# Routing the first group of the last mixture-of-experts phase inside the attention cycles ahead of it

## The reference

```
x = x + tanh(g_xattn[3]) * attention3(layernorm(x), ctx)      # phase 6
x = x + tanh(g_ffn[3])   * moe3(layernorm(x))                 # phase 7, the last

# moe3: 32 experts of 64 hidden units, in 8 groups of 4
scores = sigmoid(h @ gate_w.T);  sc = scores + gate_bias
group_scores = sum of the top 2 of each group; keep the best 4 groups
masked = sc where kept, else 0;  tki = top 8 of masked
tkw = scores[tki] / (sum + 1e-20) * 2.5
out = sum over experts of tkw * ((silu(h w_gate) * (h w_up)) w_down) + shared expert
```

## Time and profile before

| | |
|---|---|
| three timed runs | 866.33, 873.83, 873.89 us; median 873.83 |
| the profiled execution | 869.13 us, its span 867.3 us, so 1.8 us lie around the span |
| TensorE busy | 824.7 us (95%) |
| VectorE, GpSimd, ScalarE busy | 515.7, 471.2, 407.0 us |
| mean granted TensorE clock | 0.985 of full speed |

### The profile page before, as it was taken

One profiled execution on the slowest core, in us unless ns is written; L12 is line 12 of the kernel. 1 busy time (PEld: TensorE's weight loads), 2 busy tenths in 40 slices (PEclk: granted clock), 3 DMA queues, 4 the chain that ended last, 5 costly groups with the idle time before them and its releaser, 6 DMA issues.

```text
span 867.3 us, 13578 instructions
## 1 busy us (share of the span) xinstructions
PE 824.7 (95%) x4427; PEld 560.2 (65%) x4427; DVE 515.7 (59%) x1444; ACT 407.0 (47%) x730; POOL 471.2 (54%) x449
## 2 busy tenths in 40 slices
PE   5999999998899999999998999999999988999997
PEld 5866676665566666665765666656566665666664
DVE  6866645584865646335555868686755466556431
ACT  2343353634436242325666676756556633424231
POOL 5585757465573747476444343354545248475553
PEclk9999999999999999999999999999999899999999
DMA  8303111214313142441323131322223024424251
GB/s 317 104 15 99 63 36 32 85 43 154 119 44 119 62 129 67 136 124 35 89 83 107 46 89 42 95 50 50 55 49 93 1 67 134 147 66 148 75 154 50
DMA packets 44727, 75.29 MB, mean 87 GB/s; under 512 B 8977, under 2 KB 9361, under 8 KB 44529
## 3 DMA queue, kind: packets, MB, share of 16 engines
q1 hardware_dynamic: 44512, 74.42, 28.4%
q10 hardware_dynamic: 144, 0.01, 0.0%
HBM read 56.11 MB, written 1.51 MB: 66 GB/s over the span
## 4 chain that ended last, share of the span: by engine, by line
PE 56%; DVE 9%; ACT 3%; issue 2%; POOL 0%; ACTq 0%; DVEq 0%; POOLq 0%
PE Y L930 13%; PE B L857 6%; PE B L855 6%; PE B L856 6%; PE B L1498 5%; PE B L1517 3%; PE B L1479 3%; PE B L1485 2%; PE Y L1370 2%; PE B L1478 2%; DVE mxh L1768 1%; PE T L1303 1%; DVE xhat L1752 1%; DVE bcs L1943 1%; ACT shared L1379 1%
## 5 line engine op out<-in xcount | busy, mean ns | idle before, releaser
L1172 POOL TENSOR_TENSOR shared<-shared,bcs 128x512 f32<-128x512 f32 x192 | 247.4, 1293 | 195.8 <-DVE shared L1209 177.0
L1209 DVE TENSOR_TENSOR shared<-shared,B 128x512 f32<-128x512 f32 x204 | 139.5, 686 | 206.4 <-PE B L857 160.4
L1058 ACT ACTIVATE shared<-B 128x512 f32<-128x512 f32 x204 | 121.7, 598 | 280.0 <-PE B L857 279.5
L930 PE MATMUL Y<-shared,down_lo 128*128 128x512 f32 x408 | 209.1, 598 | 0.0
L1712 POOL TENSOR_TENSOR shared_r<-shared_r,const 128x512 fp32r<-128x512 f32 (+1 forms) x128 | 116.4, 940 | 80.3 <-PE B L1479 61.8
L1768 DVE TENSOR_REDUCE mxh<-B 128x4 fp32r<-128x512 f32 (+1 forms) x128 | 78.9, 618 | 82.2 <-PE B L1479 81.5
L1648 ACT COPY shared<-B 128x512 f32<-128x512 f32 (+1 forms) x128 | 64.7, 505 | 61.6 <-PE B L1498 61.5
L1638 ACT ACTIVATE shared<-B 128x512 f32<-128x512 f32 (+1 forms) x128 | 69.6, 544 | 48.9 <-PE B L1485 47.6
L930 PEld LDWEIGHTS Y<-shared,down_lo 128*128 128x128 f32 x408 | 72.5, 190 | 21.1 <-issue 9.5
L855 PE MATMUL B<-shared_r,gate_hi 128*128 128x512 f32 x102 | 80.9, 794 | 0.0
L855 PE MATMUL B<-x_lo_r,gate_hi 128*128 128x512 f32 x102 | 77.6, 761 | 0.4 <-ACT shared L1058 0.4
(11 more groups left out here) (306 smaller groups left out, 1469.8 us busy)
## 6 DMA issues: line engine op xcount, KB each, us to landing
bcs<-wrow SPq DMA_DIRECT2D x96, 256.0 KB, 3.8
shared_r<-shared_r SPq DMA_DIRECT2D x256, 64.0 KB, 2.0
bcs<-wrow SPq DMA_DIRECT2D x128, 128.0 KB, 2.9
gate_lo<-in_moe SPq DMA_DIRECT2D x9, 256.0 KB, 5.3
up_lo<-in_moe SPq DMA_DIRECT2D x9, 256.0 KB, 5.5
down_lo<-in_moe SPq DMA_DIRECT2D x9, 256.0 KB, 4.3
small<-in_small SPq DMA_DIRECT2D x1, 1372.5 KB, 11.7
X<-in_x SPq DMA_DIRECT2D x4, 256.0 KB, 5.2
```

The lines of the kernel that those rows point to most:

```text
L930: nc.tensor.matmul(Y[:], w_raw[2][:, at:at + P], hid[(n0 + c) % HIDDEN], start=(i == 0), stop=(i == m["NC"] - 1))\
L1058: nc.scalar.activation(sg[(n0 + n) % ACTIVE], B[n % GATES][:], ACT.Silu).then_inc(sem("sg_ready"), 1)
L1172: gp.tensor_tensor(hid[(n0 + n) % HIDDEN], hid[(n0 + n) % HIDDEN], bcs[(PLACE.k0[p] + r // m["PER"]) % BROADCAST], ALU.mult)\
L1209: nc.vector.tensor_tensor(hid[(n0 + n) % HIDDEN], sg[(n0 + n) % ACTIVE], up[:], ALU.mult)\
```

## The change

Group 0 of phase 7 is taken through everything up to its router row before the second stream begins. In cycle 6 DVE takes its statistics at t = 10 and applies them at t = 14, POOL's power for it is moved behind the key spreading of the next cycle's first quarter. In cycle 7 a new table `FINAL` puts `rows` at t = 1 and `result` at t = 15, and `ROUTE` puts the low part at t = 2, the logits at 3, an exponential on ACT at 4, the seven pieces of the routing on DVE at 5 to 11, the turn at 12 and the row's copy at 13. The sigmoid of this one group becomes exp(-x) on ACT, and an addition of 1 and a reciprocal on DVE. Group 1's statistics come at t = 14 of cycle 7 in place of chunk 4. In the stream, `xt` of group 1 moves from chunk 7 to chunk 1 and its logits from chunk 9 to 6; the leftovers of phase 6 shift from chunks 1, 2, 3 to 3, 4, 5. Context lines are cut:

```
@@ -640,6 +640,11 @@
             dve.wait_ge(sem("logits_read"), PLACE.no[p] + g + 1)
+            if (p, g) == (7, 0):
+                st.add(v.tensor_scalar(t["sig"][:], t["sig"][:], 1.0, None, ALU.add))
+                st.settle()
+                st.add(v.reciprocal(t["sig"][:], t["sig"][:]))
+                st.settle()
             st.add(v.tensor_tensor(t["s"][:].rearrange("p (j n) e -> p j (n e)", j=GB), t["sig"][:],
@@ -701,7 +706,7 @@
                     if (p, g) == (7, 0):
-                        table.update(xt=7, logits=9)
+                        table.update(xt=1, logits=6)
                     if (p, g) == (1, 0):
@@ -991,23 +996,24 @@
                         back_pe(pe, 6, QUADS * NG - 1)
-                    elif (p, n) == (7, 1):
-                        pe.wait_ge(sem("logits_read"), PLACE.no[7] + 1)
+                    elif (p, n) == (7, 3):
+                        pe.wait_ge(sem("x_lo_ready"), PLACE.no[7] + 2)
                         upsample_pe(pe, NG - 1)
-                    elif (p, n) == (7, 2):
+                    elif (p, n) == (7, 4):
                         pe.wait_ge(sem("up_ready"), NG)
                         heads_turned_pe(pe, 6, NG - 1)
-                    elif (p, n) == (7, 3):
+                    elif (p, n) == (7, 5):
                         output_pe(pe, 6, NG - 1)
-                    elif (p, n) == (7, 5):
-                        turn(7, 0)
                 G = run.hook("xt", n)
...
                     p, g = run.groups[G]
-                    pe.wait_ge(sem("w_row_ready"), PLACE.no[p] + g + 1)
+                    if (p, g) == (7, 0):
+                        pe.wait_ge(sem("x_updated"), s - 1)
+                    else:
+                        pe.wait_ge(sem("w_row_ready"), PLACE.no[p] + g + 1)
                     normed(s + 1)
@@ -1022,6 +1028,8 @@
                     pe.wait_ge(sem("x_lo_ready"), PLACE.no[p] + g + 1)
+                    if (p, g) == (7, 1):
+                        pe.wait_ge(sem("heads_oT_ready"), CYCLES)
                     logits(p, g)
@@ -1058,12 +1066,10 @@
                     turned_act(act, 1)
-                elif (p, n) == (7, 2):
+                elif (p, n) == (7, 4):
                     heads_turned_act(act, 6, NG - 1)
-                elif (p, n) == (7, 4):
+                elif (p, n) == (7, 6):
                     result_act(act, 6, run.step(0) - 1)
-                elif (p, n) == (7, 6):
-                    turned_act(act, 7)
                 H = run.hook("xt", n - 1)
@@ -1193,8 +1199,7 @@
             else:
-                pieces = route_dve(dve, st, 7)
-                next(pieces)
+                pieces = iter(())
             setup = setup_dve(dve, st)
@@ -1210,12 +1215,8 @@
                     divided_dve(dve, st, 6, QUADS * NG - 1)
-                elif (p, n) == (7, 1):
+                elif (p, n) == (7, 3):
                     upsample_dve(dve, NG - 1)
-                elif (p, n) == (7, 4):
-                    norm_stats(st, 1)
-                if (p, g) == (7, 0):
-                    next(pieces, None)
                 for kq, what in (("q", "query"), ("k", "key")):
@@ -1453,8 +1454,11 @@
 
+        FINAL = dict(rows=1, key=8, query=11, result=15, value=4)
+        ROUTE = dict(low=2, logits=3, exp=4, first=5, turn=12, row=13)
+
         def steps_of(c):
-            return LATER if c else FIRST
+            return FIRST if c == 0 else LATER if c + 1 < CYCLES else FINAL
 
@@ -1524,7 +1528,7 @@
                 else:
-                    pe.wait_ge(sem("heads_oT_ready"), c)
+                    pe.wait_ge(sem("x_updated"), S4 + c - 1)
                 pe.wait_ge(sem("xhat_ready"), S4 + c + 2)
@@ -1535,7 +1539,7 @@
                 else:
-                    pe.wait_ge(sem("xhat_t_ready"), S4 + c + 2)
+                    pe.wait_ge(sem("w_row_ready"), PLACE.no[7] + 1)
                 for j in range(GB):
@@ -1556,7 +1560,7 @@
                         else:
-                            pe.wait_ge(sem("x_updated"), S4 + c - 1)
+                            pe.wait_ge(sem("logits_read"), PLACE.no[7] + 1)
                         upsample_pe(pe, c - 1 - NG)
@@ -1592,9 +1596,11 @@
                         values_pe(pe, *group(c + 1))
-                    if t == 15 and c + 1 == CYCLES:
-                        pe.wait_ge(sem("x_updated"), S4 + c)
+                    if t == ROUTE["logits"] and c + 1 == CYCLES:
                         route_pe(pe, 7)
+                    if t == ROUTE["turn"] and c + 1 == CYCLES:
+                        pe.wait_ge(sem("heads_oT_ready"), c)
+                        turn_pe(pe, 7)
                     slots_pe(pe, c, t)
@@ -1623,6 +1629,12 @@
                             x_high_act(act, 7)
+                    if t == ROUTE["exp"] and c + 1 == CYCLES:
+                        act.wait_ge(sem("logits"), PLACE.no[7] + 1)
+                        nc.scalar.activation(route[7]["sig"][:], logits_of(7), ACT.Exp, scale=-1.0)\
+                            .then_inc(sem("logits_read"), 1)
+                    if t == ROUTE["row"] and c + 1 == CYCLES:
+                        turned_act(act, 7)
                     if t == at["query"] and c + 1 < CYCLES:
@@ -1651,7 +1663,6 @@
                     os_act(act, group(q // QUADS)[0], q % (QUADS * NG))
-            scores_act(act, 7)
 
@@ -1731,13 +1742,15 @@
                 one_head_pool(pool, *group(c), 2)
-                if c:
+                if c and c + 1 < CYCLES:
                     power(S4 + c + 1)
...
                     one_head_pool(pool, *group(c + 1), 0)
+                if c + 2 == CYCLES:
+                    power(S4 + CYCLES)
                 if 1 <= c <= NG:
@@ -1758,6 +1771,7 @@
 
+            pieces = route_dve(dve, st, 7)
             for n in range(ALL):
@@ -1785,12 +1799,20 @@
                 divide(n)
-                if t == 5 and c:
+                if t == 5 and 0 < c < CYCLES - 1:
                     norm_stats(st, (c + 1) % NG)
-                if t == 9 and c:
+                if t == 9 and 0 < c < CYCLES - 1:
                     apply(S4 + c + 1)
-                if t == 12 and c + 1 == CYCLES:
+                if t == 10 and c + 2 == CYCLES:
+                    norm_stats(st, 0)
+                if t == 14 and c + 2 == CYCLES:
+                    apply(S4 + CYCLES)
+                if t == ROUTE["low"] and c + 1 == CYCLES:
                     x_low_dve(dve, 7)
+                if t >= ROUTE["first"] and c + 1 == CYCLES:
+                    next(pieces, None)
+                if t == 14 and c + 1 == CYCLES:
+                    norm_stats(st, 1)
             divide(ALL + 1)
```

## The result

The changed kernel takes 861.57 us (median of 6 executions, 857.81 to 864.66), the kernel before 873.32 us (6 executions, 866.33 to 874.49): a ratio of 0.9874, 95% interval 0.9846 to 0.9903. In a second set it was 860.73 against 873.01 us, 0.9856 (0.9829 to 0.9882). The forecast of 864.5 lies 2.9 us from the first; the gain of 1.26% is over the 1% to which I gave 0.35, where 0.60 stood on "within 1%".

What follows compares the result with a forecast made beforehand. PE was taken as the bound, so time is won only from its waits, lower clock or unneeded work. Stream 7.2 less cycles 1.2 gives 6.0 us: 863.1 from the profile, 865.5 from the middle execution, 864.5 taken; range 857 to 872.

Steps and rivals of the forecast that it cites:

- within 1%: Whole kernel: time changes by less than 1% (8.7 us), about what a measurement cannot tell from none; chance 0.60.
- Group 1's rows: Stream: with earlier statistics, PE's wait for POOL's normalised rows goes, with slack of 2 us or more; gain 2.3 us.
- Group 1's routing: Stream: logits at chunk 6 end PE's router-row wait at chunk 15, 3.0 us, and the clock fall after it, 1.55 us.
- The broadcast, costed at nothing: Stream: group 0's row is broadcast about 24 us earlier, so POOL's weighting starts on time; PE never waited, gain nothing.
- The rule of the Trainium skill that I had held against the change: Cycle 7: DVE and GpSimd share a port pair under an exclusive lock, holding PE up by 2 to 4 us more.
- Rival 2: Cycle 7, t = 5 to 11: DVE becomes the bound beside POOL, costing 2 to 4 us, 867 to 868; chance 0.14.
- The cycles: Cycles 6 and 7: added turn, routing, statistics, apply and copies cost net 1.2 us, bounds -0.5 and +4.
- Rival 1: End of cycle 7: the clock does not fall at 687.5 us, 3.0 us more gain, 861.5; chance 0.28.
- the likeliest case: Whole kernel: the forecast itself, a gain of 4 to 8.7 us; chance 0.50.
- 7.2 were forecast: Stream's sum: 2.3 + 3.0 + 1.55 + 0.44 + 0.3 gained, 0.4 lost to a new wait at chunk 3.

Runs made afterwards that it cites:

- experiment 3: Kernel before with group 1's statistics after chunk 1's side steps instead of chunk 4's: 870.80 us, ratio to before 0.9971.
- experiment 7: Kernel before with group 0's router logits in cycle 7 at t = 13 instead of 15: 876.69 us, ratio to before 1.0025.
- experiment 5: Changed kernel with group 1's logits back at chunk 9 and its routing pieces two to a chunk: 865.84 us, ratio to before 0.9910.
- experiment 8: Changed kernel with group 0's router row broadcasts held until chunk 5's product, as late as before the change: 864.82 us, ratio to before 0.9904.
- experiment 2: Kernel before with the turn of group 1's router row at chunk 16 instead of 15: 870.34 us, ratio to before 0.9963.
- experiment 9: Kernel before with group 0's router logits moved from cycle 7 to after the stream's first chunk: 872.70 us, ratio to before 0.9983.
- experiment 6: Changed kernel with POOL's splitting of the last weights in cycle 7 held until group 0's router row is ready: 861.25 us.
- experiment 10: Changed kernel with group 0's logits computed once more at t = 15 of cycle 7, into a bank nobody reads: 861.86 us.

## Why the prediction was right, and where it was wrong

*Group 1's rows, 2.3 us.* The wait went, and slack was as forecast. Taken alone (experiment 3) the term gave 2.2 us in the median. That profile's longer wait for the row, 4.8 us, is no proof that the two terms overlap, since experiment 7 has 4.7 with the POOL wait still there.

*Group 1's routing, 3.0 + 1.55 us.* The sum was nearly met (wait 3.0 to 0.7, clock up), the reason was wrong. I wrote that the pieces occupied chunks 10 to 16, and described one piece after each chunk's product. They did not: the first group's chunks ran two pieces each, so the row was due at chunk 13, two ahead of the turn. It came late because DVE was behind. In before's profile the first piece starts 27.8 us after the stream's first chunk, PE asks for the row 10.1 us later, and DVE needs 13.0 us to `comb`, 12.3 of them busy with the pieces, the next statistics, a result and the products. In the changed kernel the first piece starts at 16.8 us, PE asks 16.0 us later, and DVE needs 16.6:

```profile
717.88 0.29 DVE L643 TENSOR_TENSOR s<-sig,small 128x128 f32<-128x128 f32 x1 [0.77 <-ACT sig L890]
730.55 0.30 DVE L613 SCALAR_TENSOR_TENSOR comb<-w,rec 128x128 f32<-128x128 f32 x1
```

```profile
710.08 0.80 DVE L648 TENSOR_TENSOR s<-sig,small 128x128 f32<-128x128 f32 x1 [0.76 <-ACT sig L895]
726.40 0.28 DVE L613 SCALAR_TENSOR_TENSOR comb<-w,rec 128x128 f32<-128x128 f32 x1
```

In the changed layout two things keep the wait short, each needed: the logits three chunks earlier (experiment 5: 4.25 us of the first group without them) and POOL's early weighting (experiment 8: 3.6 us).

*"The broadcast, costed at nothing."* This is the step that failed. PE did not wait for the rows, but DVE's small instructions did take longer beside POOL, and the late rows of experiment 8 make POOL work with hardly a pause: seven of group 1's routing instructions take 0.7 to 1.3 us there, where they take 0.2 to 0.3 with POOL idle. Five do in the changed kernel too (0.8 to 1.3 us). The routing's 39 instructions take 11.4 us together in the changed kernel and 13.4 in experiment 8, 2.1 more, and PE's wait is 1.9 longer; the rest of the 3.6 us is the clock that falls behind it. How much of this the old layout paid is not shown: there they took 9.2 us in before's profile, less than after the change, and 11.3 to 13.1 in experiments 2, 3, 7 and 9. The rule of the Trainium skill that I had held against the change (page "SBUF — State Buffer", section "Who interferes with whom": an exclusive lock for a whole instruction) speaks for it in the stream. Experiments 6 and 8 agree with it as far as they go: the time added to one DVE instruction (0.70, 0.95 and 1.10 us) stays below one POOL instruction (1.27 us).

*Rival 2, the same rule in cycle 7,* did not come: the stretching was there and cost nothing (experiment 6).

*The cycles, +1.2 us.* Measured +1.3 without a fall of the clock. Cycle 6, to which I had given half, paid 0.2. Cycle 7 paid 1.1, against a before that had a fall in its drain; against experiment 9's 28.4, with no logits in it and no fall, it is 2.9. Addition and reciprocal took 1.17 us, not 0.5.

*Rival 1, the clock at the seam, 0.28.* It held, and so the likeliest case, which left it out, was not the one that came. In four of four profiles with the layout of before and logits at t = 13 or 15 it fell, at 684 to 688 us; in experiment 9, without them, and in all nine profiles of the changed kernel and its variants it did not fall there. That accounts for about 2 us of the first group (4.1 us at half clock) and 1 in the drain, which I had left out of the likeliest case. With logits in the tail it fell in each profile of the old layout, without them in the one there is not, and in the new one they are not enough (experiment 10). What else in the new tail keeps the clock up stays open.

*The size.* In the first group 9.0 us came where 7.2 were forecast, the rest being the seam's clock. The medians moved by 6 us more than the profiles say. Before's profiled execution was a good one, 869.1 us, 4.2 below its median, and experiment 7 shows the same stream at 48.7 instead of 45.7 us; the changed kernel's was a poor one, 1.8 above its median, with the fall at 661. I had seen that the profile lay 4.7 us below the median, took the middle, and did not ask which wait could be longer in the others. That the time still came out 2.9 us from the forecast is in part luck: the seam's clock and the early rows had no term in the sum, and the start was put halfway between the profile and the median.

Falls in the changed stretch are no fixed cost: the one at 661 us was there in the profiles of the first run and of experiment 8, and absent in seven other variants.

## What to carry to other kernels

A row that comes late can cost through the engine that must catch up: here its back-to-back instructions stretched another engine's small ones, and the wait for that engine is the one that showed. When a wait is removed, ask why the waited-for engine is late, not only where it is asked; moving the question by a chunk gave 2.7 us in the median here, moving the work gave 9 us of the first group. And where the profiled execution is well below the median, read its waits as lower bounds.

## What was unexpected of the hardware

A DVE instruction on 128x32 elements took 0.18 us beside an idle POOL and up to 1.28 us beside a busy one; three additions on 128x96, 128x64 and 128x32 took 0.52 us beside an idle POOL and 1.60, 1.81, 2.75 and 3.83 us (experiment 3) beside a busy one. A reciprocal on 128x128 took 0.95 us where a multiplication of that size took 0.29. A wait of 0.4 us before the same instructions was followed by a fall of TensorE's granted clock in one execution and not in another, while a wait of 1.0 us in cycle 7 was followed by none in seven profiles. By the estimate above, half of the whole gain (7 of 12 us) is a clock that is lower for less of the time.
